# Mixer B's output projection and norms moved into its chunk loop, its first norm into the stage before, and one activation table for logarithm and exponential

## The chip, the cores and the metric

The program runs on one core of a Trainium2 chip. Such a core has five engines with a queue of instructions each: TensorE (PE, matrix products into the accumulator memory, here `ps`, eight banks of 128 x 512 float32), VectorE (DVE), ScalarE (ACT, functions by table), GpSimd (POOL) and SyncE (SP, which issues transfers). They run beside each other and wait for each other by semaphores. The metric is the time on the device in microseconds (us), the median of several runs.

## The reference

Four blocks follow each other, each on `x = x + block(layernorm(x))`, with `x` of 2 x 1024 tokens by 128 channels: mixer A (a selective state-space scan with state 16), an FFN with a shared expert and eight routed ones, mixer B, and the same FFN again. The change is about mixer B, cut here to what matters:

```python
h = rmsnorm(u, norm_w)                    # u = layernorm(x)
z, xBC, dt = split(h @ in_proj_w.T)       # 256 | 512 | 4 channels
xBC = silu(conv4(xBC) + conv_b)           # xs (4 heads x 64), B (128), C (128)
dt = softplus(dt + dt_bias);  A = -exp(A_log)
step: h = h * exp(dt*A) + dt * x (outer) B;   y = h @ C    # over 128 tokens
y = y + D * xs
y = rmsnorm(y * silu(z), ssm_norm_w)
x1 = u + y @ out_proj_w.T
h = rmsnorm(x1, post_norm_w)
return x1 + (silu(h @ gate_w.T) * (h @ up_w.T)) @ down_w.T
```

The residual of the network adds this to `x`.

## The kernel before

Everything lies as channels on the 128 partitions and T = 2048 tokens in the free dimension, worked on in four pieces of CH = 512 tokens (`cols(c)`, NCH = 4). Five stages follow each other, each one a block with one hand-written list of instructions per engine: loading, `mixer_a_stage` (0 to 280.5 us in the trace), `ffn_stage` with tag f (to 641.3), `mixer_b_stage` (641.6 to 818.9) and `ffn_stage` with tag g. No scheduler sets an order: each engine runs its list in the order of the code, and semaphores join the lists. A function of the same name often stands in the lists of several engines.

Mixer B, in the order of its lists. `Norm` (lines 188 to 233) centres x by a matmul (L194), squares it on ACT (L204), sums by a matmul (L188), and makes two logarithms a piece on ACT: the joint one (layer norm and RMS norm in one, L212) and the plain one (L214); then exponentials (L218, L221) and multiplications on DVE (L233) and POOL. The projections (L1787, L1810) follow, and DVE's convolution (L2205, L2208) in six passes. Then the chunk loop: TT = 16 chunks of 128 tokens. `chunk_inputs(c+1)` on PE makes the decay exponents and transposes of the next chunk (L1836, L1825, L1827, L1844 to L1846), ACT's `chunk` exponentiates (L2004, L2009, L2011) and `keep` decays the state (L2016), DVE's `prepare` and `next_state` mask, scale and add (L2240 to L2267), POOL scales the values by dt (L2189) and builds the step matrices two chunks ahead (L2160), and `chunk_outputs(c)` on PE makes y of the chunk (L1860, L1861) and its state (L1864). Behind every fourth chunk `gate_y` on DVE (L2274, L2282) adds D*xs and multiplies by silu(z), ACT squares (L2024), PE sums the squares (L1873, `mean_squares`), and ACT saves the sum (L2028).

Behind the loop come the output projection (`project_out`, L1879), logarithm and exponential for both norms (L2093 to L2118), the residual (L2327, L2329), the sum of its squares (L1943), the scaling (L2333), the split of the input into a high and a low part for rounded matmuls (`high_of_x` L2032, `low_of_x` L2287), and the MLP in NQ = 12 steps: gate and up matmuls (three passes each, L1884 to L1886), silu (L2128), product (L2344), and two steps later the down matmuls.

ACT's functions come in table sets, and a change of set is an instruction of its own, ACT_TABLE_LOAD. Log stands in the set `natural_log`, exp in `exp_and_others`, silu in `silu_and_others`. In the whole program there are 42 such loads.

In an FFN stage, a shared expert runs in a loop over q (`down(q - 2)`), then 39 tiles of gathered rows run through the experts: POOL gathers rows by indirect transfers, `turn_row` transposes them on PE (L1141), and ACT and DVE make silu(gate)*up (L1299, L1618) for the two halves of each tile. DVE's `add(2)` (L1579) is the last addition of the shared expert.

## Time and profile before

| what | value |
|---|---|
| runs, us | 1187.43, 1183.34, 1183.73 (median 1183.73) |
| profiled execution, us | 1191.55 |
| its span, first to last instruction | 1189.7 |
| busy PE / DVE / ACT / POOL, us | 994.6 / 742.7 / 601.5 / 594.8 |
| mean granted clock of PE | 0.923 of full |
| instructions | 16179 |
| mixer B from its first instruction | 641.6 to 818.9 us of the span |

The span is the time from the first to the last instruction; the execution's own time is 1.85 us longer. Busy time is the sum over an engine's instructions. Idle time is put down to what ended it ("<-"). A granted clock of 1.00 is 2.4 GHz, of 0.50 it is 1.2 GHz. `x4` behind a row says that so many equal instructions that follow each other are in it, with the sum of their time. A float32 matmul is two passes, each counted as one.

### The profile page before, as it was taken

The numbers are of one execution on the slowest core, as the hardware profiler recorded it, in microseconds if no ns is written. First come the engines' busy times: TensorE is split into PE (matmuls) and PEld (weight loads), VectorE is DVE, ScalarE is ACT, GpSimd is POOL, SyncE is SP. The second block draws the span as 40 slices with busy tenths as digits, with TensorE's granted clock in tenths as the row PEclk, the third lists the DMA queues.
The fourth block names the chain that finished last, engine by engine and source line by source line (L and its number), as shares of the span: only waits on it lengthen the run. The fifth ranks groups of instructions, "written<-read, shape, count | busy, mean of one in ns | idle before, by whom it ended". The sixth has DMA issues, their size and how long they took to land. (4 is left out here: it accounts for less than half of the span.)

```text
span 1189.7 us, 16179 instructions
## 1 busy us (share of the span) xinstructions
PE 994.6 (84%) x4707; PEld 704.7 (59%) x4707; DVE 742.7 (62%) x1197; ACT 601.5 (51%) x1129; POOL 594.8 (50%) x465
## 2 busy tenths in 40 slices
PE   5889999988996779973997888878996679993698
PEld 2323333335666669973985456455665669993696
DVE  4899999995873436641655866554683336651466
ACT  5675657656332435531556766667432335551353
POOL 2388988995048653364114746211128543547212
PEclk8999899989998889995999879988998889996899
DMA  4222222335011231121004000004111212111003
GB/s 131 64 72 71 82 80 83 96 92 170 19 59 38 71 70 52 54 73 35 15 12 111 1 1 1 1 0 135 54 60 28 77 31 90 56 52 51 19 12 113
DMA packets 60399, 69.40 MB, mean 58 GB/s; under 512 B 6232, under 2 KB 42848, under 8 KB 60320
## 3 DMA queue, kind: packets, MB, share of 16 engines
q1 hardware_dynamic: 55328, 58.15, 16.2%
q0 software_dynamic: 4992, 10.23, 3.3%
q8 instruction: 46, 0.75, 0.3%
q14 instruction: 33, 0.27, 0.1%
HBM read 57.74 MB, written 10.62 MB: 57 GB/s over the span
## 5 line engine op out<-in xcount | busy, mean ns | idle before, releaser
L764 POOL TENSOR_TENSOR a_hc<-a_h,a_c_sb 128x512 f32<-128x512 f32 x128 | 159.5, 1268 | 41.0 <-DVE a_h L672 40.9
L449 PE MATMUL ps<-a_hc,eye 128*128 128x512 f32 x256 | 133.6, 637 | 9.8 <-POOL a_hc L764 8.8
L589 ACT ACTIVATE ps<-a_delta,a_neg_a 128x512 f32<-128x512 f32 x128 | 87.3, 688 | 64.1 <-DVE a_h L672 63.5
L1126 PE MATMUL ps<-f_ring_rounded,f_q_hi_rounded 128*128 x312 | 81.8, 352 | 25.7 <-DVE f_q_hi_rounded L1591 17.2
L1126 PE MATMUL ps<-g_ring_rounded,g_q_hi_rounded 128*128 x312 | 80.3, 347 | 22.4 <-DVE g_q_hi_rounded L1591 22.4
L449 PEld LDWEIGHTS ps<-a_hc,eye 128*128 128x128 f32 x256 | 45.1, 194 | 77.1 <-POOL a_hc L764 40.1
L1618 DVE TENSOR_TENSOR g_prods<-g_work,ps 128x470 f32<-128x470 f32 x78 | 50.1, 644 | 53.7 <-remote 32.1
L672 DVE TENSOR_TENSOR_SCAN a_h<-ps,a_state,a_b_u 128x512 f32<-128x512 f32 x64 | 78.7, 1266 | 3.8 <-ACT ps L589 3.6
L1126 PEld LDWEIGHTS ps<-f_ring_rounded,f_q_hi_rounded 128*128 128x128 f32 x312 | 62.1, 199 | 29.6 <-issue 27.1
L1618 DVE TENSOR_TENSOR f_prods<-f_work,ps 128x470 f32<-128x470 f32 x78 | 50.0, 644 | 46.3 <-remote 23.4
L672 DVE TENSOR_TENSOR_SCAN a_h<-ps,a_b_u 128x512 f32<-128x512 f32 x64 | 75.2, 1207 | 3.1 <-ACT ps L589 2.9
L1299 ACT ACTIVATE g_work<-ps 128x470 f32<-128x470 f32 x78 | 43.8, 563 | 65.8 <-remote 35.7
L1126 PEld LDWEIGHTS ps<-g_ring_rounded,g_q_hi_rounded 128*128 128x128 f32 x312 | 61.0, 196 | 26.3 <-issue 23.8
L974 POOL CAST g_ring_rounded<-g_ring 128x1876 fp32r<-128x1876 f32 x8 | 14.0, 1754 | 122.5 <-DMA g_ring<-in_dn 122.5
L1299 ACT ACTIVATE f_work<-ps 128x470 f32<-128x470 f32 x78 | 43.7, 564 | 54.9 <-PE ps L1157 31.6
L1108 PE MATMUL ps<-eye,g_prods 128*128 128x128 f32 x312 | 44.1, 288 | 32.4 <-DVE g_prods L1618 32.4
L1003 POOL DMA_INDIRECT token_rows<-f_rows,f_back x39 | 37.8, 968 | 66.9 <-DVE f_rows L1597 59.1
L1003 POOL DMA_INDIRECT token_rows<-g_rows,g_back x39 | 37.4, 960 | 64.0 <-DVE g_rows L1597 55.9
L652 DVE TENSOR_TENSOR a_b_u<-a_du,ps 128x1024 f32<-128x1024 f32 x57 | 68.0, 1194 | 0.1
L1587 DVE TENSOR_TENSOR g_q_lo_rounded<-ps,g_q_hi_rounded 128x512 fp32r<-128x512 f32 x78 | 45.8, 620 | 34.5 <-ACT g_q_hi_rounded L1276 20.0
L995 POOL DMA_INDIRECT g_rows<-xn_rows,g_source x39 | 37.0, 949 | 58.2 <-DVE g_source L1545 47.1
L1155 PE MATMUL ps<-f_ring_rounded,f_work_rounded 128*128 x156 | 63.9, 409 | 1.7 <-issue 0.9
(483 smaller groups left out, 2902.5 us busy)
## 6 DMA issues: line engine op xcount, KB each, us to landing
a_c_sb<-c_rows SPq DMA_DIRECT2D x64, 256.0 KB, 3.2
f_ring<-in_gu SPq DMA_DIRECT2D x16, 469.0 KB, 4.3
g_ring<-in_gu SPq DMA_DIRECT2D x16, 469.0 KB, 4.2
f_ring<-in_dn SPq DMA_DIRECT2D x8, 512.0 KB, 5.9
g_ring<-in_dn SPq DMA_DIRECT2D x8, 512.0 KB, 5.6
xn_rows<-f_work SPq DMA_DIRECT2D x8, 256.0 KB, 3.6
f_rows<-token_rows SPq DMA_DIRECT2D x8, 256.0 KB, 5.2
xn_rows<-g_work SPq DMA_DIRECT2D x8, 256.0 KB, 2.8
```

The source lines that it names most:

```text
L449: nc.tensor.matmul(ps[:, Y + f, :], k.eye[:, :], hc[:, s % WAITING, :], start=False, stop=(n == NST - 1)).then_inc(y_added, 1)
L589: nc.scalar.activation(ps[:, A + m % NA, :], delta[:, f, cols(g)], ACT.Exp, scale=neg_a[:, f, n:n + 1])\
L652: nc.vector.tensor_tensor(decayed_in[:, p:p + FT, :], du[:, :, cols(g)], ps[:, B + i % 2, :].unsqueeze(1).to_broadcast([P, FT, CH]), ALU.m ...
L672: nc.vector.tensor_tensor_scan(h[:, s % DEPTH, :], ps[:, A + m % NA, :], decayed_in[:, m % FEED, :], initial, ALU.mult, ALU.add).then_inc( ...
L764: nc.gpsimd.tensor_tensor(hc[:, m % WAITING, :], h[:, s % DEPTH, :], c_sb[:, i % RING, :], ALU.mult)\
L1003: nc.gpsimd.indirect_dma_start(k.token_rows, bass.IndirectOffsetOnAxis(ap=back[:, j:j + 1], axis=0), rows[:, j, :], None).then_inc(sent, 16)
L1108: last = nc.tensor.transpose(ps[:, TR + i // 4, (i % 4) * P:(i % 4 + 1) * P], prods[:, j % 2, i * P:(i + 1) * P], k.eye[:, :])
L1126: last = nc.tensor.matmul(ps[:, Y2, 0:2 * P], q_hi[:, j % 2, a], in_ring(place, w, w + 2 * P), start=(i == 0), stop=(i == NI), skip_group_ ...
L1155: nc.tensor.matmul(out, xt[:, 0, j % 2, :], w_hi, start=True, stop=False)
L1299: nc.scalar.activation(gates[:, half, 0:HALVES[half]], ps[:, 2 * half, 0:HALVES[half]], ACT.Silu)\
L1587: last = nc.vector.tensor_tensor(q_lo[:, j % 2, a], ps[:, TR + half, 0:n], q_hi[:, j % 2, a].bitcast(F32), ALU.subtract)
L1618: nc.vector.tensor_tensor(prods[:, j % 2, half * H0:half * H0 + HALVES[half]], gates[:, half, 0:HALVES[half]], ps[:, 2 * half + 1, 0:HALVE ...
```

## The change

It has six parts.

- One table set, `LOG_EXP`, holds logarithm and exponential, and takes the place of the other two everywhere in both mixers. There are 22 table loads then.
- Mixer B's first norm (centring, squares, sums, joint logarithm) runs at the end of stage f, in the lists `centre_next`, `variance_next`, `square_next`, `log_next`, with f's additions as its input. Mixer B's weights are loaded there too, on SP. The plain norm's logarithm comes in the convolution, its exponential in chunks 0 to 3, the multiplication on POOL there.
- The output projection, both norms and the residual run inside the chunk loop, piece by piece. There are five pieces: 512, 512, 512, 256 and 256 tokens, which end with chunks 4, 8, 12, 14 and 16 (`PIECES`, `ENDS`). The sums, the projection and the variance of one piece use one bank in turn (`turn_of`).
- The last chunk's state, which nobody reads, isn't made.
- The multiplication in `gate_y` is one instruction over both banks.
- In both FFN stages `turn_row(0)` stands one step earlier on PE, and DVE's `add(2)` stands ahead of the waits for the first tile's second half.

```diff
+LOG_EXP = "natural_log_exp_and_others"
...
     (ffn_stage, PE)
+                if q == NPRE - 1:
+                    turn_row(0)
                 if q >= 2:
                     down(q - 2)
-            turn_row(0)
...
     (ffn_stage, DVE)
                 for half in range(2):
+                    if j == 0 and half:
+                        add(2)
                     dve.wait_ge(gates_silu, 2 * j + half + 1)
                     dve.wait_ge(ups_ready, 2 * j + half + 1)
-                    if j == 0 and half:
-                        add(2)
...
     (end of ffn_stage f, ACT)
+            if following is not None:
+                def square_next(c):
+                    act.wait_ge(next_centred, c + 1)
+                    nc.scalar.activation(work[:, cols(c)], ps[:, NEXT_CENT[c], :], ACT.Square).then_inc(next_squared, 1)
+                def log_next(c):
+                    act.wait_ge(next_var, c + 1)
+                    nc.scalar.activation(following.joint[:, cols(c)], ps[:, NEXT_VAR[c], :], ACT.Ln, bias=k.eps[:, 2:3])
...
     (mixer_b_stage)
+    PIECES = [slice(c * CH, (c + 1) * CH) for c in range(NCH - 1)]
+    PIECES += [slice(T - CH, T - CH // 2), slice(T - CH // 2, T)]
+    ENDS = (4, 8, 12, 14, 16)
+    def turn_of(p):
+        return ps[:, S if p == ALL - 1 else M, 0:width(p)]
...
     (PE)
+            def variance(p):
+                pe.wait_ge(res_done, p + 1)
+                pe.wait_ge(n_squared, p + 1)
+                nc.tensor.matmul(turn_of(p), k.ones[:, :], y[:, 0, PIECES[p]], start=True, stop=True)\
+                    .then_inc(n_ready, 1)
             for c in range(TT):
                 if c + 1 < TT:
                     chunk_inputs(c + 1)
+                if c in (8, 12):
+                    variance(c // 4 - 2)
                 chunk_outputs(c)
-                if c % 4 == 2 and c > 4:
+                if c in (4, 8, 12):
                     mean_squares(c // 4 - 1)
+                if c in (5, 9, 13):
+                    project_out(c // 4 - 1)
+                if c == 14:
+                    variance(2)
+            mean_squares(3)
+            gate_up(0)
+            project_out(3)
+            mean_squares(4)
+            gate_up(1)
+            project_out(4)
+            variance(3)
+            variance(4)
...
     (ACT, behind chunk(c) and keep(c - 1))
+                if c < NCH:
+                    act.wait_ge(plain_log, 1)
+                    nc.scalar.activation(rms[:, c, :], rms[:, c, :], ACT.Exp, scale=-0.5).then_inc(plain_ready, 1)
+                if c in (9, 13):
+                    rstd_n(c // 4 - 2)
+                if c in (5, 9, 13):
+                    square(c // 4 - 1)
+                if c in (6, 10, 14):
+                    rms_of(c // 4 - 1)
+                if c in (7, 11, 15):
+                    square_n(c // 4 - 1)
+                if c in (10, 14):
+                    high_of_x(c // 4 - 2)
+            square(3); rstd_n(2); rms_of(3); square(4); rms_of(4)
+            square_n(3); rstd_n(3); square_n(4); rstd_n(4)
             nc.scalar.preload_act_table_set("silu_and_others")
+            high_of_x(2)
...
     (DVE, behind next_state(c + 1))
-                if c % 4 == 3:
+                if c in (3, 7, 11):
                     gate_y(c // 4)
+                if c == 13:
+                    gate_y(3)
+                    residual(2)
+                if c in (5, 9):
+                    residual(c // 4 - 1)
+                if c in (9, 13):
+                    scale_in(c // 4 - 2)
+                if c in (10, 14):
+                    low_of_x(c // 4 - 2)
+            gate_y(4); scale_in(2); residual(3); residual(4)
+            low_of_x(2); scale_in(3); scale_in(4)
```

How the lists look now at two places. First ACT around chunks 9 and 10 (an exponential, a copy and an exponential, then `b_kept`, are one chunk). Before, a square stood ahead of chunk 9, and chunks 9 and 10 followed each other:

```order
L2024 ACTIVATE b_sq<-b_y 128x1024
L2004 ACTIVATE ps<-ps 128x512
L2009 ACTIVATE b_toks<-ps 128x384
L2011 ACTIVATE ps<-ps 128x512
L2016 ACTIVATE b_kept<-b_state,b_e_end 128x64 x4
L2004 ACTIVATE ps<-ps 128x512
L2009 ACTIVATE b_toks<-ps 128x384
L2011 ACTIVATE ps<-ps 128x512
L2016 ACTIVATE b_kept<-b_state,b_e_end 128x64 x4
```

After, from the end of chunk 9 (line numbers of the changed kernel: L2136 and L2138 are `rstd_n`, L2120 `square`, L2125 and L2127 `rms_of`, L2142 `high_of_x`):

```order
L2112 ACTIVATE b_kept<-b_state,b_e_end 128x64 x4
L2136 ACTIVATE b_raw_b<-ps,eps 128x512
L2138 ACTIVATE b_raw_b<-b_raw_b 128x512
L2120 ACTIVATE b_sq<-b_y 128x1024
L2100 ACTIVATE ps<-ps 128x512
L2105 ACTIVATE b_toks<-ps 128x384
L2107 ACTIVATE ps<-ps 128x512
L2112 ACTIVATE b_kept<-b_state,b_e_end 128x64 x4
L2125 ACTIVATE b_rms<-ps,eps 128x512
L2127 ACTIVATE b_rms<-b_rms 128x512
L2142 ACTIVATE b_sz_rounded<-b_xp 128x512
```

Six instructions stand between chunks now, three behind chunk 9 and three behind chunk 10; of these only the square was in the loop before.

Second, PE at the loop's end. Before, behind the last chunk's y and state: all projections, the last sum of squares, all variances, then the MLP:

```order
L1861 MATMUL ps<-b_c_in,b_state 64x128
L1864 MATMUL ps<-b_x_end,b_toks 128x256
L1879 MATMUL ps<-b_y,b_w_out 128x512 x6
L1873 MATMUL ps<-b_sq,half 128x512 x2
L1879 MATMUL ps<-b_y,b_w_out 128x512 x2
L1943 MATMUL ps<-b_y,ones 128x512 x4
L1884 MATMUL ps<-b_sz_rounded,b_w_hi 128x512
```

After (L1951 `mean_squares`, L1970 to L1972 one product of the MLP, L1959 `project_out`, L1966 `variance`):

```order
L1937 MATMUL ps<-b_c_in,b_state 64x128
L1951 MATMUL ps<-b_sq,half 128x256 x2
L1970 MATMUL ps<-b_sz_rounded,b_w_hi 128x512
L1971 MATMUL ps<-b_sz_rounded,b_w_hi 128x512
L1972 MATMUL ps<-b_sz_rounded,b_w_lo_rounded 128x512
L1970 MATMUL ps<-b_sz_rounded,b_w_hi 128x512
L1971 MATMUL ps<-b_sz_rounded,b_w_hi 128x512
L1972 MATMUL ps<-b_sz_rounded,b_w_lo_rounded 128x512
L1959 MATMUL ps<-b_y,b_w_out 128x256 x2
L1951 MATMUL ps<-b_sq,half 128x256 x2
```

The projections of three pieces are gone from here; the last two pieces, of half width, stand between the products of the MLP's first two steps.

## Rows read from the trace of the kernel before

**Rows 1.** Windows: from:to, length, busy us of PE, PEld, DVE, ACT, POOL, then PEclk.

```profile
346.00:619.00 273.00, 220.84 (x1401) 203.11 (x1400) 129.54 (x275) 111.18 (x235) 134.14 (x101) 0.89 0.16 46
...
694.00:765.00 71.00, 62.82 (x444) 44.77 (x445) 45.93 (x96) 46.62 (x119) 37.64 (x44) 0.95 0.00 1
765.00:819.00 54.00, 42.38 (x136) 27.55 (x134) 28.19 (x44) 36.17 (x57) 5.07 (x4) 0.91 0.00 0
```

**Rows 2.** Time line, 19 to 23 us: start, length, line, count, [idle before <-releaser].

```profile
19.89 1.28 ACT L218 ACT_TABLE_LOAD   x1
21.19 2.19 ACT L218 ACTIVATE a_du<-a_du 128x512 f32<-128x512 f32 x4
...
22.79 1.19 PE L351 MATMUL ps<-a_xp,a_w_tap 128*128 128x512 f32 x1 [5.11 <-DVE a_xp L233]
```

**Rows 3.** Waits of DVE, 40 to 310 us: us in total, times, longest.

```profile
DVE a_h L672 <- ACT ps L589: 6.6, 6, 2.0
```

**Rows 4.** Time line in mixer A's scan loop, 150 to 153 us.

```profile
150.62 1.28 ACT L568 ACT_TABLE_LOAD   x1
...
152.64 1.28 DVE L672 TENSOR_TENSOR_SCAN a_h<-ps,a_state,a_b_u 128x512 f32<-128x512 f32 x1 [2.04 <-ACT ps L589]
```

**Rows 5.** Chain that ended last, first norm of g: start, length, what.

```profile
823.67 1.28 ACT L1245
```

**Rows 6.** Time line, first expert tile of stage f.

```profile
352.21 0.69 DVE L1579 TENSOR_TENSOR x<-x,ps 128x512 f32<-128x512 f32 x1 [1.32 <-PE ps L1157]
...
353.04 0.30 PE L1141 MATMUL ps<-eye,f_rows 128*128 128x128 f32 x1 [0.93 <-DVE x L1579]
```

**Rows 7.** Time line, beginning of mixer B.

```profile
641.60 1.28 ACT L206 ACT_TABLE_LOAD   x1 [4.09 <-PEq L922]
...
650.96 1.28 ACT L218 ACT_TABLE_LOAD   x1
...
653.75 3.75 PE L1787 MATMUL ps<-b_xp,b_w_in 128*128 128x512 f32 x4 [5.00 <-DVE b_xp L233]
...
657.54 1.28 DVE L2205 TENSOR_SCALAR b_bc<-ps,vec 128x1024 f32<-128x1024 f32 x1 [2.14 <-PE ps L1787]
```

**Rows 8.** Page, part 5: costliest groups (count | busy, mean ns | idle before).

```profile
L764 POOL TENSOR_TENSOR a_hc<-a_h,a_c_sb 128x512 f32<-128x512 f32 x128 | 159.5, 1268 | 41.0 <-DVE a_h L672 40.9
```

**Rows 9.** Time line of TensorE in the chunk loop.

```profile
708.64 0.38 PE L1836 MATMUL ps<-b_bc 128*128 128x128 f32 x2
...
711.83 0.38 PE L1836 MATMUL ps<-b_bc 128*128 128x128 f32 x2
...
715.12 0.45 PE L1860 MATMUL ps<-b_mix,b_x_dt 128*64 128x128 f32 x4 [1.65 <-DVE b_y L2282]
```

**Rows 10.** Windows in the chunk loop, columns as in rows 1.

```profile
696.30:702.70 6.40, 6.39 (x28) 4.91 (x29) 3.18 (x8) 2.62 (x7) 4.66 (x6) 0.50 0.00 0
702.70:715.00 12.30, 10.77 (x88) 8.04 (x86) 9.14 (x20) 7.29 (x21) 7.83 (x9) 1.00 0.01 2
```

**Rows 11.** Time line, tail of mixer B and first steps of its MLP.

```profile
760.44 0.44 PE L1861 MATMUL ps<-b_c_in,b_state 128*64 128x128 f32 x4
...
761.35 5.31 PE L1879 MATMUL ps<-b_y,b_w_out 128*128 128x512 f32 x12
...
774.69 5.20 PE L1943 MATMUL ps<-b_y,ones 128*128 128x512 f32 x8 [4.60 <-ACT b_y L2111]
...
787.15 0.60 ACT L2128 ACTIVATE b_gate<-ps 128x512 f32<-128x512 f32 x1 [0.58 <-PE ps L1886]
...
788.20 0.63 PE L1884 MATMUL ps<-b_sz_rounded,b_w_hi 128*128 128x512 f32 x1
...
788.62 0.63 PE L1885 MATMUL ps<-b_sz_rounded,b_w_hi 128*128 128x512 f32 x1
...
791.96 0.60 ACT L2128 ACTIVATE b_gate<-ps 128x512 f32<-128x512 f32 x1 [0.65 <-PE ps L1886]
```

**Rows 12.** Waits of TensorE in f's expert tiles: us in total, times, longest.

```profile
PE ps L1108 <- DVE f_prods L1618: 23.7, 4, 16.0
```

More of the change, by code:

```diff
@@ L789, in mixer_a_stage, with ffn_stage @@
     return counters, spent
-def ffn_stage(k, d, which, tag, cleared, ready, out=None, logs=None):
+def ffn_stage(k, d, which, tag, cleared, ready, out=None, logs=None, following=None):
     nc, ps = k.nc, k.ps
@@ L2048, in keep_next @@
                 nc.scalar.activation(logs[:, c, :], ps[:, NEXT, :], ACT.Copy).then_inc(next_read, 1)
-            norm.of_scalar(act)
-            act.wait_ge(loaded, 48)
+            for c in range(NCH):
+                nc.scalar.activation(xp[:, cols(c)], xp[:, cols(c)], ACT.Exp, scale=-0.5).then_inc(joint_ready, 1)
             nc.scalar.activation(neg_a[:, :], head_rows[:, 1, :], ACT.Exp).then_inc(a_ready, 1)
@@ L2082, in _ @@
             for c in range(TT):
-                if c % 4 == 1 and c > 4:
-                    square(c // 4 - 1)
-                if c % 4 == 0 and c > 4:
-                    save(c // 4 - 2)
                 chunk(c)
@@ L2120, in _ @@
+                if c in (10, 14):
+                    high_of_x(c // 4 - 2)
+            square(3)
+            rstd_n(2)
+            rms_of(3)
+            square(4)
+            rms_of(4)
+            square_n(3)
+            rstd_n(3)
+            square_n(4)
+            rstd_n(4)
             nc.scalar.preload_act_table_set("silu_and_others")
-            high_of_x(1)
+            high_of_x(2)
             for q in range(NQ):
```

327 lines of the change are left out of this document (185 added, 142 removed).

## The prediction

> **What bounds the kernel now.** I read the busy time by stretch first [rows 1]: the expert tiles of f alone are 273 us (those of g as much), and the change hardly touches them. In mixer B's chunk loop (694 to 765) TensorE is busy 62.8 of 71 us, in the tail and MLP behind it 42.4 of 54. So the loop has little room to take work and the tail has much idle time to give. Then, engine by engine, the waits and the time lines around each edit, to see which engine everybody waits for there; each table load in them is 1.28 us.
>
> The sum is made against the profiled execution, 1191.55 us (span 1189.7 and 1.85 around it). The median of the three timed runs is 1183.73, 7.8 less; the terms below are differences, and I put them on the median.
>
> **Table loads with one log/exp set (42 become 22).** A load costs time only where it stands on the path.
> Start of mixer A: Ln ends at 19.88, load until 21.17, Exp, DVE's scaling, and TensorE had been idle for 5.11 us at 22.79 [rows 2]. All in one chain: -1.3. The two loads before the first scan (39 and 42 us) have ACT slack in front of them: 0.
> In mixer A's scan loop DVE sets the pace. It waited for ACT's L589 six times, 6.6 us in all, once 2.04 at 152.64 [rows 3, 4]. That one stands right behind two loads (the second at 150.62) that go; their 2.56 exceed the wait. The same pair precedes a wait of 0.19 and one of 0.61. These three add to 2.8, and I take -2.8. The other three waits stand behind silu loads and the next norm's work, which stay. Bounds: 0 if other ACT work or POOL's multiplies (159.5 us [rows 8]) are what ends a round, -6.6 if all waits went.
> The loads at mixer A's end lie beside DVE work, and so does the one in f's first norm: 0. In g that norm's load is on the path: in the chain that ended last the load stands from 823.67 to 824.95 [rows 5]. -1.3 (bounds 0 and -1.3).
>
> **Add and turn moved in the FFN stages.** At tile 0 DVE's add (L1579) sat behind the wait for the second half: it began at 352.21 after 1.32 idle, and TensorE waited 0.93 for it [rows 6]. Ahead of the waits it fills that idle time; L1618 then starts some 0.65 sooner, since the next instruction starts 0.60 behind the add's start. -0.7 in each of f and g, -1.4 together (0 to -1.9, twice the wait). The gather behind turn_row(0) is governed by its DMA, not by the matmuls around it: 0, at worst 0.3 each way.
>
> **Mixer B's first norm at the end of f.** Before, the block begins with a load (641.60); behind squares and Ln comes a second load (650.96), Exp, DVE's scaling, TensorE's projections (3.75 for four, half clock) and at 657.54 DVE's convolution [rows 7]. After, centring can start behind f's last transposes, some 1.4 sooner, since only the additions of f are needed; both loads are off the chain (the first preloads while ACT waits, as ACT had idled 4.09). The four joint Ln no longer have the four plain ones (0.57 each) between them, but the block's change now falls between Ln and Exp, and DVE does two copies of 0.7 and w_in 0.6 ahead of its scaling. My walk, an estimate: logs end at 647.85, 0.35 for the block's change, Exp 648.2, scaling from 650.05, convolution from 653.9 at full clock or 654.65 at half. 657.54 - 654.65 = 2.9. Bounds -1 (if the change of block costs 2 more) and -3.7 at full clock. The plain norm's Ln lies beside DVE's convolution, and its multiply goes to POOL in chunks 0 to 3, 1.27 us each by the 128x512 multiplies of [rows 8]. POOL is busy 7.83 of 12.30 us in the second row of [rows 10]; four more make 12.9, just too much, but POOL has idle time before the loop: 0 to +0.8, taken as 0 within the loop's term.
>
> **The chunk loop takes the output projection and norms.** A steady chunk is 3.18 us (708.64 to 711.83) with TensorE back to back [rows 9], so each matmul put in is paid: three projections 5.31 (twelve passes, 0.44 each [rows 11]); three variances at two passes 2.6; one dropped state matmul -0.5; the three mean_squares only move. That is +7.4 of TensorE alone. Then waits. PE now asks for square(p) right behind chunk 4p+4 and for variance(p) at 8 and 12, while ACT has square, Ln, Exp and high_of_x queued between its chunks, and DVE residual, scale_in and low_of_x. ACT's in-order queue is the danger: high_of_x at c=10 waits for scale_in, behind it stand the three exponentials of chunk 11, and for these wait DVE's mix and TensorE. Walking the queues with the durations of such rows gives groups of four chunks longer by 1.7, 3.4 and 5.4 us to the last y: +10.5, of which 2.65 is one wait of TensorE, for square_n(2) ahead of variance(2). The gate, for which TensorE sat idle 1.65 at 715.12, stays. Bounds: +6 if DVE's single 128x1024 multiply and shorter idle times before chunks give some back; +20 if each of the nine pieces of ACT and DVE work (3 x square, Ln/Exp, residual) pushes its chunk by its own 1.1 to 1.4 us.
>
> **The tail.** Before: last y ends about 760.85, first silu of the MLP (L2128) at 787.15, 26.3 us [rows 11]. In it are the projections (5.31), four loads (5.1) and a round of eight Ln, eight Exp and residuals at full width, with TensorE idle 4.60 in front of the variances. After it, counted from the last y: gate of half a piece 1.7; TensorE meanwhile does mean_squares(3) and gate_up(0), six passes at 0.43 (788.20 to 788.62, clock at half there), then project_out(3) and mean_squares(4), to 5.3; Ln and Exp at half width 0.9; two DVE halves 1.0; square 0.4; variance and its wait 0.6; Ln and Exp 0.9; silu load 1.28; high_of_x 0.6; first silu at 11.45 (sum with handovers of 0.5). That is -14.85. The first two MLP steps' matmuls are then done: before, the third silu came 4.81 behind the first, after 3.5: -1.3. Bounds of the two together: -12 (each handover 0.3 more, everything at half clock) and -18 (full clock, and the ACT queue short).
>
> **Sum.** -1.3 - 2.8 - 1.3 - 1.4 - 2.9 + 10.5 - 14.85 - 1.3 = -15.35. 1183.73 - 15.35 = 1168.4. I say 1168.5 (for the profiled execution 1176).
>
> **Two rules of the skill.** A load is followed at once by the next instruction: load from 19.89, 1.28 long, Exp at 21.19 [rows 2]. The Trainium skill, "ScalarE: Activation LUTs", section "What ACT_TABLE_LOAD costs", gives the same 1.28 us for the load but adds a drain of about 1.38. By it each of six loads on the path (one at the start, one at mixer B's front, three net in the tail, one in g) would give 1.38 more, an estimate of -23 to -24 in all; the row shows no such gap, and I don't count it.
> Idle TensorE has cost its clock here: the stretch 696.3 to 702.7, behind the convolution in which TensorE had little to do, ran at 0.50, 1.2 GHz, and its chunk took 6.4 us instead of 3.18; the chunks behind it ran at 1.00, 2.4 GHz, and the idle 1.65 at 715.12 is followed by passes of full speed [rows 9, 10]. The Trainium skill, "TensorE: Matmul & The Clock Gate", section "HAM oscillation — how this bites in real kernels", warns that stalls inside a loop can throw the engine back to half rate again and again; this speaks against putting waits in the loop and is the second rival.
>
> **Rivals.**
> (1) The loop gives it all back: growth at its upper bound 20 and the tail at -12, with the other terms at -7: +1, so 1178 to 1187. For it: TensorE is busy 88% of the loop and ACT already 46.6 of 71 us [rows 1]. Against: ACT and DVE keep 24 and 25 us of idle time there, and each is asked to take some 12.
> (2) Slower: TensorE's clock falls in the loop. New waits stand at six places (squares at 4, 8, 12, variances at 8, 12, 14). Each fall costs 3.2 us as at 696.3. With +10.5 and -25.85 for the rest, five falls give +0.65, and at six with the loop's waits at their upper bound (+9.5) it is 1183.73 - 15.35 + 19.2 + 9.5 = 1197. It decides from five or six falls. Against: the three waits of 1.6 us there now cause none.
> (3) The expert stages shift. In f's expert tiles TensorE waits 23.7 us in four times for DVE, once 16.0 [rows 12], and in g likewise; DVE and ACT stand still there too. What sets them off isn't in the profile; if their number depends on where instructions fall, one more or less moves the time by 7 to 16 us, and the spread of the times (1183.3 to 1191.6) may be this. One less: 1152 to 1161; one more: 1176 to 1184.
> (4) The loads are hidden anyway: without the 5.4 us of table terms 1174.
>
> **How the numbers follow.** Forecast 0.5, rival 1 0.14, rival 2 0.05, rival 3 0.09 up and 0.07 down, rival 4 0.15. What a measurement can tell from no change is 0.5%, 5.9 us, so faster is below 1177.8. The forecast, rival 4 and the lower shift are faster (0.72), and of the upper shift about half: 0.77. Rival 1 mostly and the rest of rival 3: same 0.16. Rival 2 and the tail of rival 1: slower 0.07. The forecast's own terms sum to bounds of roughly -22 to -6; with the shifts and a part of rival 1 the range is 1157 to 1180.
>
> **What would show it.** ACT's loads 22, the DVE wait at 152 gone; the convolution 3 us sooner after f's last addition; from the last y to the MLP's first silu 11 to 12 us instead of 26; the loop from its first y to its last longer by 8 to 13 with a granted clock of 1.0; no idle TensorE of over 3 us in the tail. Wrong if the loop's stretches show a clock of 0.5, if TensorE waits over 3 us at the variances, or if the expert stretches differ from before's (273 us in f) by more than 3 us.

## The result, and the profile after

| | before | after |
|---|---|---|
| median of 16 timed runs, us | 1186.46 | 1178.24 |
| lowest and highest | 1179.95, 1193.67 | 1172.11, 1183.86 |
| span of the profiled execution | 1189.7 | 1182.1 |

The ratio is 0.993, with a 95% interval of 0.9908 to 0.9952: the change takes 8.2 us (5.7 to 10.9) where I had forecast 15.3. The sign was right and the size was not. (The forecast counted from 1183.73, the median of three runs; sixteen give 1186.46.)

I cut both traces at the same events and compare the pieces. The windows of the changed kernel, with its columns as in [rows 1], from y of chunk 0 to chunk 4, on to y of the last chunk, to the MLP's first silu, to its last matmul, to the first matmul of g's gate, and to g's first expert tile:

```profile
691.80:707.90 16.10, 14.12 (x109) 10.73 (x108) 10.69 (x22) 12.29 (x35) 15.74 (x18) 0.95 0.01 1
707.90:765.00 57.10, 48.61 (x319) 31.12 (x319) 38.34 (x74) 35.90 (x88) 27.11 (x31) 1.00 0.01 1
765.00:779.50 14.50, 10.28 (x49) 8.04 (x48) 3.87 (x8) 7.84 (x16) 3.02 (x3) 0.86 0.00 0
779.50:809.60 30.10, 29.01 (x104) 20.82 (x104) 19.00 (x32) 18.28 (x35) 0.00 (x0) 0.90 0.00 1
809.60:816.70 7.10, 3.78 (x9) 1.27 (x8) 1.39 (x3) 4.66 (x7) 0.00 (x0) 1.00 0.62 202
816.70:884.70 68.00, 65.47 (x270) 47.56 (x270) 48.92 (x99) 26.66 (x44) 15.64 (x10) 0.92 0.28 87
```

and the same pieces of the kernel before:

```profile
698.90:715.10 16.20, 14.57 (x109) 11.27 (x108) 10.69 (x23) 8.84 (x27) 10.29 (x12) 0.88 0.01 2
715.10:759.70 44.60, 39.88 (x300) 28.41 (x300) 29.57 (x63) 29.69 (x78) 24.59 (x29) 1.00 0.00 1
759.70:787.10 27.40, 17.19 (x51) 8.42 (x51) 10.96 (x17) 21.26 (x30) 5.07 (x4) 0.89 0.00 1
787.10:817.80 30.70, 30.47 (x114) 22.22 (x112) 19.14 (x31) 18.72 (x34) 0.00 (x0) 0.93 0.00 1
817.80:826.40 8.60, 3.82 (x10) 1.30 (x9) 1.47 (x3) 6.11 (x9) 0.00 (x0) 0.95 0.70 221
826.40:892.00 65.60, 63.72 (x270) 45.92 (x270) 48.86 (x99) 26.64 (x44) 15.74 (x10) 0.95 0.27 84
```

The loop from chunk 4 on went from 44.6 to 57.1 us; TensorE is busy 8.7 us more in it (48.6 against 39.9) and idle 3.8 us more. The tail went from 27.4 to 14.5, the MLP from 30.7 to 30.1, g's norm from 8.6 to 7.1, and the stretch behind that grew from 65.6 to 68.0 at a lower clock (0.92 against 0.95). In front of the loop, the new beginning of mixer B, which answers to [rows 7]:

```profile
645.34 2.19 ACT L2161 ACTIVATE b_xp<-b_xp 128x512 f32<-128x512 f32 x4 [0.33 <-PEq L924]
...
647.14 2.47 DVE L2422 TENSOR_TENSOR b_xp<-ps,b_xp 128x512 f32<-128x512 f32 x4
...
647.96 2.68 PE L1859 MATMUL ps<-b_xp,b_w_in 128*128 128x512 f32 x4 [3.69 <-DVE b_xp L2422]
...
650.73 1.27 DVE L2307 TENSOR_SCALAR b_bc<-ps,vec 128x1024 f32<-128x1024 f32 x1
```

DVE scales x 9.93 us after f's last transposes (637.21 to 647.14); before it was 12.71 (640.21 to 652.92). The convolution starts at 650.73, TensorE's four passes in front of it (2.68 us) at a length between the 1.96 of full and the 3.75 of half clock (both are shown with e1 and e8).

In the first mixer the wait of [rows 3] has shrunk, and two others beside it have grown; before, a_yz stood at 4.0 and a_b_u at none:

```profile
DVE a_yz L632 <- PE ps L452: 5.0, 6, 1.7
DVE a_h L670 <- ACT ps L588: 3.6, 3, 1.8
...
DVE a_b_u L650 <- PE ps L439: 0.8, 1, 0.8
```

And the waits of TensorE in the loop:

```profile
PE ps L1936 <- DVE b_y L2382: 3.2, 3, 1.3
PE ps L1966 <- ACT b_y L2132: 2.6, 1, 2.6
PE ps L1959 <- ACT b_rms L2125: 2.1, 3, 0.7
PE ps L1899 <- DVE b_mix L2346: 1.1, 2, 0.7
PE ps L1899 <- POOL b_steps_lo L2261: 0.9, 2, 0.5
```

The first is the gate, smaller than before (4.8, the same three). The second is the one I had expected at 2.65, ahead of variance(2). The 2.1 are new: three times 0.69 in front of a projection. So are the 0.9 for POOL.

At the end of the loop ACT, DVE and TensorE stand like this:

```profile
759.60 0.69 DVE L2395 TENSOR_TENSOR b_xp<-xn,b_raw_b 128x512 f32<-128x512 f32 x1
...
760.32 0.63 ACT L2142 ACTIVATE b_sz_rounded<-b_xp 128x512 fp32r<-128x512 f32 x1 [3.59 <-DVE b_xp L2395]
...
760.85 0.58 ACT L2100 ACTIVATE ps<-ps 128x512 f32<-128x512 f32 x1
...
763.21 0.62 ACT L2132 ACTIVATE b_y<-xn 128x512 f32<-128x512 f32 x1
...
763.97 1.10 PE L1966 MATMUL ps<-b_y,ones 128*128 128x512 f32 x2 [2.62 <-ACT b_y L2132]
...
764.99 0.64 PE L1936 MATMUL ps<-b_mix,b_x_dt 128*64 128x128 f32 x4
...
765.39 0.66 PE L1937 MATMUL ps<-b_c_in,b_state 128*64 128x128 f32 x4
...
774.27 0.43 DVE L2389 TENSOR_TENSOR ps<-ps,b_rms 128x256 f32<-128x256 f32 x1 [2.23 <-PE ps L1959]
...
777.67 1.28 ACT L2221 ACT_TABLE_LOAD   x1
...
779.50 0.58 ACT L2229 ACTIVATE b_gate<-ps 128x512 f32<-128x512 f32 x1
```

ACT's high_of_x (L2142) waits 3.59 us for DVE's scaling, and only behind it come the exponentials of the last chunk (L2100) and the square (L2132) that TensorE's variance (L1966) waits for. The two y passes at 764.99 and 765.39 take 0.64 and 0.66 instead of 0.45: the granted clock has fallen to half (0.53 from 765.0 to 766.9). In the tail the first silu (L2229) comes at 779.50, 12.6 us behind the last y, with DVE's residual at 774.27 and the load at 777.67 on its way, as in the forecast's walk. At the beginning of the MLP TensorE stands idle 3.53 us (to 780.22) for that silu, where I had allowed none over 3.

### The profile page after: what moved, and what is told of

Its sections match the earlier page's. It is cut to its first block and busy times, and to the rows that moved or that the text cites. A ratio compares the mean times of both kernels' runs of the same rounds, so it can differ in the third digit from the quotient of the medians.

```text
span 1182.1 us, 16202 instructions
## 1 busy us (share of the span) xinstructions
PE 1004.1 (85%) x4715; PEld 712.0 (60%) x4715; DVE 745.9 (63%) x1204; ACT 573.3 (49%) x1109; POOL 595.7 (50%) x465
## 5 line engine op out<-in xcount | busy, mean ns | idle before, releaser
L452 PE MATMUL ps<-a_hc,eye 128*128 128x512 f32 x256 | 135.0, 645 | 10.3 <-POOL a_hc L762 9.7
L1134 PE MATMUL ps<-f_ring_rounded,f_q_hi_rounded 128*128 x312 | 81.8, 352 | 23.4 <-DVE f_q_hi_rounded L1639 15.3
L452 PEld LDWEIGHTS ps<-a_hc,eye 128*128 128x128 f32 x256 | 46.3, 198 | 77.4 <-issue 38.7
L1645 DVE SCALAR_TENSOR_TENSOR g_rows<-ps,g_share,g_work 128x128 f32<-128x128 f32 x39 | 13.7, 350 | 87.5 <-ACT g_work L1310 84.8
L1163 PE MATMUL ps<-g_ring_rounded,g_work_rounded 128*128 x156 | 65.1, 417 | 0.5 <-issue 0.5
```

The lines of the kernel that those rows point to most:

```text
L452: nc.tensor.matmul(ps[:, Y + f, :], k.eye[:, :], hc[:, s % WAITING, :], start=False, stop=(n == NST - 1)).then_inc(y_added, 1)
L1134: last = nc.tensor.matmul(ps[:, Y2, 0:2 * P], q_hi[:, j % 2, a], in_ring(place, w, w + 2 * P), start=(i == 0), stop=(i == NI), skip_group_ ...
L1163: nc.tensor.matmul(out, xt[:, 0, j % 2, :], w_hi, start=True, stop=False)
```

## The experiments

Each is timed against the kernel before on its own chip. The chip of e1, e2, e3 and e6 runs both expert stages without the bursts of waits of [rows 12] (211 us instead of 273), so its times lie some 124 us lower; ratios and pieces outside those stages are comparable. e2 and e6 have two runs each, the others four to twelve. e6 leaves out half of three projections, so what it computes is not the result; it is there for its time alone.

| run | what | median, us | before, us | ratio (95%) |
|---|---|---|---|---|
| e1 | table set alone | 1048.83 | 1062.03 | 0.9892 (0.9863 to 0.9921) |
| e2 | changed kernel, two sets | 1085.14 | 1062.03 | 1.0221 (1.0175 to 1.0267) |
| e3 | changed kernel, queue order | 1047.87 | 1062.03 | 0.9883 (0.9853 to 0.9913) |
| e6 | changed kernel, half projections | 1048.46 | 1062.03 | 0.9875 (0.9838 to 0.9913) |
| e7 | changed kernel | 1178.17 | 1187.35 | 0.9927 (0.9900 to 0.9954) |
| e8 | table set alone | 1171.84 | 1187.35 | 0.9872 (0.9832 to 0.9911) |
| e9 | e3, later projections, silus first | 1174.00 | 1187.35 | 0.9871 (0.9826 to 0.9916) |
| e10 | e9, POOL's work spread | 1174.05 | 1187.35 | 0.9881 (0.9845 to 0.9918) |
| e11 | e3, silus first, POOL spread | 1166.43 | 1183.76 | 0.9861 (0.9832 to 0.9890) |
| e12 | e11, weights scaled in f | 1167.79 | 1183.76 | 0.9867 (0.9825 to 0.9909) |
| e13 | changed kernel without the loop's part | 1173.80 | 1186.57 | 0.9910 (0.9878 to 0.9942) |
| e14 | changed kernel | 1177.98 | 1186.57 | 0.9938 (0.9915 to 0.9960) |
| e15 | e13, POOL spread, silus first | 1170.91 | 1186.57 | 0.9889 (0.9857 to 0.9920) |
| e16 | e11 again | 1169.79 | 1186.57 | 0.9886 (0.9853 to 0.9919) |

The pieces of the traces, in us ("f to scaling" is from the end of f's last transposes to DVE's first scaling of x; the loop's parts run from y to y, the tail from the end of the last y, the last column from g's gate to its first tile; the last y itself stands in no column: 1.14 us, but 1.95 in after, 1.71 in e14, 2.03 in e7, e2 and e6):

| run | f to scaling | to convolution | chunks 0-4 | chunks 4-15 | tail | MLP | g's norm | g's front |
|---|---|---|---|---|---|---|---|---|
| before | 12.71 | 4.62 | 16.19 | 44.62 | 26.27 | 30.67 | 8.55 | 65.66 |
| after | 9.93 | 3.59 | 16.09 | 57.05 | 12.56 | 30.11 | 7.13 | 68.01 |
| e7 | 9.93 | 4.32 | 16.41 | 57.63 | 11.86 | 29.81 | 7.11 | 66.52 |
| e14 | 9.91 | 4.33 | 15.88 | 58.01 | 11.74 | 29.58 | 7.11 | 66.39 |
| e1 | 11.30 | 2.83 | 14.45 | 44.57 | 22.56 | 30.42 | 7.14 | 63.44 |
| e8 | 11.30 | 4.63 | 14.79 | 44.60 | 21.94 | 30.63 | 7.12 | 63.61 |
| e13 | 9.92 | 4.28 | 16.27 | 44.59 | 21.36 | 30.29 | 7.12 | 63.13 |
| e15 | 9.92 | 4.47 | 14.44 | 44.59 | 21.94 | 30.33 | 7.13 | 63.10 |
| e3 | 9.92 | 4.61 | 15.90 | 53.29 | 11.75 | 29.16 | 7.13 | 64.66 |
| e9 | 9.93 | 4.47 | 16.41 | 53.71 | 11.21 | 30.23 | 7.12 | 68.70 |
| e10 | 9.92 | 4.38 | 14.58 | 53.70 | 11.22 | 28.98 | 7.12 | 68.02 |
| e11 | 9.92 | 4.61 | 15.44 | 53.30 | 11.22 | 29.85 | 7.12 | 63.23 |
| e12 | 9.34 | 4.37 | 15.14 | 53.30 | 11.23 | 29.38 | 7.12 | 66.37 |
| e16 | 9.92 | 4.61 | 15.43 | 53.30 | 11.21 | 29.83 | 7.12 | 63.33 |
| e6 | 9.92 | 4.28 | 16.42 | 55.54 | 12.83 | 30.28 | 7.13 | 63.11 |
| e2 | 10.08 | 4.63 | 15.90 | 70.20 | 18.25 | 30.43 | 11.44 | 70.54 |

**e1 and e8, the table set alone.** The kernel before with one set and without the loads that this makes needless (22 are left):

```diff
-        nc.scalar.preload_act_table_set("natural_log")
+        nc.scalar.preload_act_table_set("natural_log_exp_and_others")
...
-                        nc.scalar.preload_act_table_set("exp_and_others")
```

> The kernel before with one log/exp table set and nothing else of the change: 22 table loads instead of 42, the order of before everywhere. The trace after showed only 1.6 us gained up to the first matmul of stage f, where I had forecast 4.1. Theory 1 (the loads were partly hidden, and the start differs by chance): f's first norm matmul 1.0 to 2.5 us earlier than in before's trace, the scan's waits for L589 down from 6.6 to about 3.6 us, TensorE's waits there up by about 1.5. Theory 2 (all of the forecast 4.1 is there, and the one trace of after was unlucky): 3.5 us or more earlier. In the tail of mixer B three loads stand on the chain: last y to first silu 22.3 to 23.8 instead of 26.3. The chunk loop unchanged within 0.3. All together 5 to 8 us below before, 1179 to 1182 by before's 1186.5.

> The kernel before with the one table set and nothing else, again, for the comparison with the changed kernel on the same chip. Expected 0.987 to 0.991 of before. Segments as in the first run of it: last addition of f's rows to the convolution 14 us, loop 60, tail 22.5.

Measured: 0.9892 and 0.9872, that is 11 and 15 us, more than the 5 to 8 expected and more than the whole change gives. The pieces say where. The tail shrinks by 3.7 and 4.3 (three loads are 3.8); f to scaling by 1.41, one load and 0.13; g's norm by 1.42. The first mixer's scan, from first scan to last, is 226.5 and 227.2 us instead of 228.7, and fourteen traces without those loads give 227.3 on average, so 1.4 and not 2.8: theory 1 of e1 on that point. The other sign fits less well: stage f began 3.1 us earlier in e1, between the two theories, and 6.6 in e8, in the range of theory 2. On average over the fourteen traces it is 3.2. The stretch from TensorE's first matmul (L351) to the first scan scatters, with the same instructions, from 19.4 (in e8) to 23.0 us, so one trace can't settle it. The beginning of mixer B in e1 and in e8:

```profile
588.07 2.48 DVE L233 TENSOR_TENSOR b_xp<-ps,b_y 128x512 f32<-128x512 f32 x4 [4.13 <-ACT b_y L218]
...
588.91 1.96 PE L1782 MATMUL ps<-b_xp,b_w_in 128*128 128x512 f32 x4 [3.59 <-DVE b_xp L233]
...
590.90 1.28 DVE L2200 TENSOR_SCALAR b_bc<-ps,vec 128x1024 f32<-128x1024 f32 x1 [0.35 <-PE ps L1782]
```

```profile
647.95 2.48 DVE L233 TENSOR_TENSOR b_xp<-ps,b_y 128x512 f32<-128x512 f32 x4 [4.29 <-ACT b_y L218]
...
648.79 3.75 PE L1782 MATMUL ps<-b_xp,b_w_in 128*128 128x512 f32 x4 [3.58 <-DVE b_xp L233]
...
652.58 1.28 DVE L2200 TENSOR_SCALAR b_bc<-ps,vec 128x1024 f32<-128x1024 f32 x1 [2.14 <-PE ps L1782]
```

The same four passes take 1.96 us in one trace and 3.75 in the other, behind the same idle time of 3.6. At full clock the convolution comes 2.83 behind the scaling and at half 4.63. The two traces are of different chips, but on e1's chip e3 and e6 have 4.61 and 4.28.

**e7, the changed kernel beside e8.**

> The changed kernel itself beside the one with the tables alone (next run). Theory 1 (the table set carries all of the gain, and moving the projection and norms into the loop gives nothing): loop, tail and MLP together were 117.8 us in the trace after and 113.2 with the tables alone, the moved first norm gives 0, the moved addition 0.7 in each FFN stage, so this one is 0 to 5 us slower than the tables alone. Theory 2 (my forecast: the moved parts are worth 16.15 + 2.9 + 1.4 - 10.5 = some 10 us, of which the tables alone can give at most 6): it is 4 us or more faster than the tables alone.

Measured 0.9927 against 0.9872 on the same chip, 6.3 us between the medians, the changed kernel the slower, somewhat more than theory 1's 0 to 5. The two intervals overlap a little (0.9900 to 0.9911), but the runs of the two kernels, compared with each other, differ by 6.2 us on average (95%: 2.1 to 10.4). e14 (0.9938) and the first timing (0.993) say the same of the changed kernel, and e1 of the tables. By the pieces the difference of the two traces is 5.9 us, and 2.9 of these stand in g's front, which none of the edits touches and whose clock was 0.95 against 1.00. Theory 1 in kind: what the change gives is the table set, and the moved parts take some of it back.

**e2, the moved parts without the one set.** One line:

```diff
-LOG_EXP = "natural_log_exp_and_others"
+LOG_EXP = "exp_and_others"
```

> The changed kernel with its logarithms and exponentials in two table sets again (61 loads instead of 22), the order of the change kept. If ACT's queue is what the loop with the norms in it hangs on (theory 1), the ten loads inside the loop (five pairs of 1.28) lengthen it by 8 to 13 us and the eight or so behind the last y lengthen the tail by 8 to 11 us: 1195 to 1205 us. If the loop is bound by TensorE alone and ACT has room for them (theory 2), the loop grows by less than 4 us and the whole is 1188 to 1194.

(The expected totals stand on before's 1186; on this chip they are 124 lower.) The loop took 88.1 us instead of 75.1, the tail 18.3 instead of 12.6: 13 and 6. The whole is 37 us slower than e3 and e6 on its chip and 23 slower than before, more than the 9 to 19 expected. In loop and tail TensorE waits 6.9, 6.3 and 6.3 us in front of mean_squares, variance and project_out. So ACT's queue has no room for loads there, and with two sets the move costs far more: theory 1, at its upper end in the loop and below it in the tail.

**e6, half of the projections in the loop.** It leaves out the other half of the first three.

```diff
-                for f in range(FT):
+                parts = range(FT) if p >= NCH - 1 else range(1)
+                for f in parts:
```

> The changed kernel with only the first half (f = 0) of each of the three projections inside the chunk loop; the second half is left out, so two passes of 0.43 each are missing three times, 2.6 us. Theory 1 (TensorE's passes put into the loop are paid one for one): first y to last y 2.2 to 3.0 us shorter than in after's trace (73.1). Theory 2 (the queues of ACT and DVE set the time of the loop): under 1 us shorter, and TensorE's waits longer by the rest.

The three chunks with a projection took 4.97, 4.96 and 4.97 us instead of 5.82, 5.82 and 5.83: 0.86 each, two passes of 0.43, paid one for one. From chunk 0 to the last y it is only 1.2 us less than in after's trace (71.96 against 73.14), because chunks 0 to 3 took 0.3 longer and the last step, with the wait for variance(2) in it, took 6.46 instead of 5.41. (Against e7 and e14 it is 2.1 and 1.9 less.) The total lies between the two theories; the passes follow theory 1.

**e3, the queue order at the loop's end.**

```diff
-                if c in (10, 14):
+                if c in (11, 15):
                     high_of_x(c // 4 - 2)
...
     (DVE; low_of_x in chunks 11 and 15 likewise)
+                if c in (9, 13):
+                    scale_in(c // 4 - 2)
                 if c == 13:
                     gate_y(3)
                     residual(2)
                 if c in (5, 9):
                     residual(c // 4 - 1)
-                if c in (9, 13):
-                    scale_in(c // 4 - 2)
```

> The changed kernel with two of its own steps moved inside the loop: DVE does scale_in ahead of gate_y and residual in chunks 9 and 13, and high_of_x and low_of_x stand in chunks 11 and 15 instead of 10 and 14, behind square_n. In the trace after, ACT stood 3.59 us at high_of_x in front of chunk 15, and TensorE then waited 2.62 us for square_n(2), after which its passes ran at half clock for some 4.5 us. Theory 1 (ACT's in-order queue makes that wait): the wait of 2.62 is gone or under 0.8, no half clock there, last y 2.5 to 4 us earlier. Theory 2 (the wait only moves to DVE's mix for the last chunk): last y within 1 us of the changed kernel's, TensorE idle in front of the last y instead.

Chunks 4 to 15 take 53.29 us instead of 57.05 to 58.01: 3.8 to 4.7 earlier, at or above the upper end of what was expected (2.5 to 4). Part of it stands at the end (the last step 3.43 instead of 5.42 in after), part at chunks 10 and 11 (3.18 and 5.11 instead of 4.38 and 6.07). TensorE's waits in loop and tail there:

```profile
PE ps L1936 <- DVE b_y L2382: 2.8, 3, 1.2
PE ps L1959 <- ACT b_rms L2125: 2.1, 3, 0.7
PE ps L1966 <- ACT b_y L2132: 2.0, 2, 1.4
```

The wait for L2132 is 0.63 in the loop (the other 1.4 are in the tail, as in the changed kernel), and the y passes behind it are at full clock. Theory 1. Loop, tail and MLP are 111.3 us then, 1.9 less than e1's 113.2, yet the timed ratio (0.9883) isn't told apart from e1's (0.9892) on the same chip.

**e9 and e10, later projections and spread POOL work.** e9 adds to e3:

```diff
+                if c in (6, 10):
+                    project_out(c // 4 - 1)
                 chunk_outputs(c)
...
-                if c in (5, 9, 13):
+                if c == 13:
                     project_out(c // 4 - 1)
...
     (DVE)
-                if c in (5, 9):
+                if c in (6, 10):
                     residual(c // 4 - 1)
...
     (ACT, ahead of the MLP loop, and DVE with low_of_x)
-            high_of_x(2)
...
     (MLP loop of ACT, and of DVE with low_of_x)
-                if q < 2:
-                    high_of_x(q + 3)
+                if q in (1, 2, 3):
+                    high_of_x(q + 1)
```

> The changed kernel with the queue order of e3, and two more moves: the projections of pieces 0 and 1 stand one chunk later on TensorE (ahead of chunk_outputs in chunks 6 and 10, DVE's residual in the same chunks), where ACT's Ln has long read the bank; and in the tail the first two silus stand ahead of high_of_x(2), which comes in MLP step 1. Theory 1 (the 0.69 in front of each projection is idle time for ACT's Ln, and TensorE's 3.5 at the MLP's begin is ACT's queue): the loop 1.2 to 1.6 us shorter than e3's 70.3, the time from the last y to the first silu 0.5 to 0.7 shorter than 11.75. Theory 2 (other waits take their place): both within 0.3 of e3's.

e10 adds to e9:

```diff
     (POOL)
-                if c < NCH:
-                    pool.wait_ge(plain_ready, c + 1)
+                if c % 4 == 0:
+                    g = c // 4
+                    pool.wait_ge(plain_ready, g + 1)
...
     (ACT and DVE: of `normed` only as much awaited as piece p needs)
```

> As e9, and POOL's four multiplications of the plain norm stand in chunks 0, 4, 8 and 12 instead of 0 to 3. With the table set alone chunks 0 to 3 take 3.18 us each and 14.45 to the fourth gate; with the multiplications in them e3 has 3.5 to 3.8 a chunk and 15.9. Theory 1 (POOL, with 3.96 us of work a chunk, sets the pace there): y of chunk 4 begins 14.5 to 15.0 us after y of chunk 0. Theory 2 (ACT's extra exponential does): still 15.5 or more. Over all this version should be the fastest: 4 to 7 us below the changed kernel.

The silus first gave 0.54 in the tail (11.75 to 11.21). The later projections gave 0.9 at chunks 6 and 10 each and lost 1.3 and 2.1 in front of chunks 8 and 12, where variance now waits for the later residual, of which the chunks behind gave back 0.6 each: 53.71 against 53.29, theory 2 in the loop and theory 1 in the tail. Spreading POOL's work brought chunks 0 to 4 from 16.41 to 14.58, which is the value of e15 (14.44) and e1 (14.45): theory 1 there. POOL in the changed kernel, chunk 1:

```profile
697.34 0.62 POOL L2288 TENSOR_TENSOR b_x_dt<-b_toks,b_dt 128x256 f32<-128x256 f32 x1
698.10 1.29 POOL L2294 TENSOR_TENSOR xn<-xn,b_rms 128x512 f32<-128x512 f32 x1 [0.15 <-ACT b_rms L2201]
699.35 1.04 POOL L2261 TENSOR_TENSOR b_steps_hi<-masks,b_dta_hi 128x512 fp32r<-128x512 f32 x1
700.35 1.04 POOL L2261 TENSOR_TENSOR b_steps_lo<-masks,b_dta_lo 128x512 fp32r<-128x512 f32 x1
```

0.62 + 1.29 + 1.04 + 1.04 with hardly an idle 0.15: 3.8 to 4.0 a chunk. As a whole e10 was 4.1 us below the changed kernel by the medians, as expected, but not the fastest: e9 has the same median, and the tables alone lie 2.2 lower.

**e11 and e12.** e11 is e3 with the silus first and the spread POOL work. e12 adds:

```diff
     (end of ffn_stage f, DVE)
-                for c in range(NCH):
+                for c in range(NCH - 1):
                     keep_centred(c)
+                dve.wait_ge(next_loaded, 48)
+                nc.vector.tensor_scalar(following.w_in[:, :], following.w_in[:, :], k.vec[:, VB_NORM:VB_NORM + 1],
+                                        (1.0 + 1e-6) ** -0.5, ALU.mult, ALU.mult)
+                keep_centred(NCH - 1)
```

> The parts of the earlier versions that paid, without the later projections, which did not (chunks 6 and 10 gained 0.9 each in e9, chunks 8 and 12 lost 1.3 and 1.9 against e3): scale_in first and high_of_x late as in e3, the two silus ahead of high_of_x(2), POOL's multiplications in chunks 0, 4, 8, 12. Theory 1 (the terms add): first y to last y 70.3 - 1.5 = 68.8 or less, last y to first silu 11.2, convolution to first y and the rest as in e10. With 0.9 less than e10: 0.985 of before, some 8 us faster than the changed kernel and 1 to 4 faster than the tables alone. Theory 2 (they don't add, a later wait takes them back): the loop 69.4 or more, not faster than the tables alone.

> As e11, and DVE scales mixer B's projection weights at the end of stage f, between two copies where it has waited 1.0 us for ACT, and no longer between the block's begin and the scaling of x. Theory 1 (the moved first norm is a chain in which DVE's copies and weights delay the scaling by 1.9): the last transposes of f to DVE's first scaling 9.3 instead of 9.9. The convolution follows 2.8 behind that at full clock of TensorE or 4.3 to 4.6 at half; which of the two comes, no theory here says. Theory 2 (ACT's exponential is what the scaling waits for): still 9.9.

e11's loop was 69.9, not 68.8, by the number in the range of theory 2: chunk 0 took 4.03 against 3.18 in e10 (the clock in chunks 0 to 3 was 0.94, against 1.00), and the rest is what was expected (53.30, as in e3). It measured 0.9861; the tables alone did not run on its chip. e12's scaling came 9.34 us behind the transposes instead of 9.92, as theory 1 has it; the time of the whole doesn't show it (0.9867).

**e13 to e16, the move into the loop by itself.** e13 is the changed kernel with before's loop and tail (`project_out`, the norms and `gate_y` as they stood, ACT's `save` with a wait for POOL's multiplications); e15 adds to it the spread (over chunks 0, 2, 4 and 6) and the silus first. On TensorE:

```diff
-                if c in (8, 12):
-                    variance(c // 4 - 2)
                 chunk_outputs(c)
-                if c in (4, 8, 12):
+                if c % 4 == 2 and c > 4:
                     mean_squares(c // 4 - 1)
-                if c in (5, 9, 13):
-                    project_out(c // 4 - 1)
-                if c == 14:
-                    variance(2)
```

> The changed kernel without its fifth part: one table set, the first norm at the end of f with its multiplications on POOL in chunks 0 to 3, the moved turn and addition; but the projection, both norms and the residual behind the loop in four full pieces, as before. Theory 1 (the move into the loop costs about what it gives): loop 62 us (60.4 and 1.6 for POOL), last y to first silu 22, to the MLP's end 30.4, together 114.5 against 117.7 of the changed kernel, so 2 to 5 us faster than it. Theory 2 (the move gives some 6 us, as forecast without the loads, and something else loses them): 5 us or more slower than the changed kernel.

> The changed kernel for the comparison on this chip: loop 75 to 76, tail 12, MLP 30; 0.991 to 0.995 of before.

> As e13, with POOL's multiplications in chunks 0, 2, 4, 6 and the first two silus of the MLP ahead of high_of_x(1), which comes in MLP step 1. Theory 1: chunks 0 to 4 take 14.5 us and the loop 60.5, last y to first silu 21.4, so 2 us faster than e13. Theory 2 (the move into the loop, tidied up as in e11, is worth having): still 1 to 3 us slower than e11, whose loop, tail and MLP take 111.

> e11 again on the same chip as the three before: loop, tail and MLP 110 to 111 us, 0.984 to 0.988 of before, the fastest of the four by 1 us or more if the terms of the traces add.

e13 is 4.2 us below e14 by the medians, within theory 1, though the intervals overlap (0.9878 to 0.9942, 0.9915 to 0.9960); the means of the two differ by 4.5 (95%: 0.1 to 9.0), and in the traces another 3.3 stand in g's front (63.13 against 66.39). By the traces loop, tail and MLP are 113.7 us without the move and 116.9 to 117.8 with it (e14, e7, after), so the move costs 3.3 to 4.1 there. Tidied up it takes 110.9 (e16), 1.5 less than e15's 112.5. The moved first norm, for its part, brings the scaling 1.4 us forward (e13 against e8), and its multiplications on POOL take 1.8 in chunks 0 to 3 until they are spread (e13 against e15). (In e15 the spread gave its 1.8 in chunks 0 to 4, and the silus first gave nothing: the tail was 21.94, not 21.4.) e15 and e16 measured 0.9889 and 0.9886, the same: the 1 us or more that was expected for e16 is below what these timings can tell, and its ratio lies a little above the expected 0.984 to 0.988. The fastest by its medians is e11 (0.9861 and 0.9886); it beats the changed kernel (8.2 us on the same chip, e16 against e14) and isn't told apart from the tables alone.

## Why the prediction came out wrong

The sum of before, term by term, against the traces of the changed kernel (after, e7, e14):

| term | forecast | measured |
|---|---|---|
| start of the first mixer | -1.3 | -1.4 on average (21.4 against 22.79 in fourteen traces, 20.5 to 22.2) |
| its scan loop | -2.8 | -1.4 |
| f's and g's addition | -1.4 | -0.7 in f and -0.6 in g (from turn_row(0) to the first L1108, after L1116: 6.76 to 6.07, 6.47 to 5.86) |
| first norm moved, to the convolution | -2.9 | -2.8 to the scaling; with the clock behind it -3.8, -3.1, -3.1 |
| loop, first y to the end of the last | +10.5 | +13.1, +14.1, +13.7 |
| tail to the first silu | -14.85 | -13.7, -14.4, -14.5 |
| MLP | -1.3 | -0.6, -0.9, -1.1 |
| g's norm | -1.3 | -1.4 |
| g's front | 0 | +2.4, +0.9, +0.7 |

**The steps that failed.** The second is the largest. First, "it waited for ACT's L589 six times ... these three add to 2.8, and I take -2.8". The wait did fall by 3.0 (6.6 to 3.6 in after, 3.0 in e7 and e8). But in the same trace DVE waited 1.0 more for TensorE's L452 and 0.8 for L439, waits for another engine that had been hidden behind the one that went. -3.0 + 1.0 + 0.8 is -1.2, and the scan took 227.5 instead of 228.7. A wait that vanishes is worth only the distance to the next engine. The bounds 0 and -6.6 held the value.

Second, the loop: "+10.5". Passes were priced rightly (e6: 0.86 for two), and so was the wait for square_n(2), 2.65 forecast and 2.62 measured. The walk had 1.7, 3.4 and 5.4 for the groups of four chunks; the traces have 1.9, 5.0 and 6.4 to 7.1. What it lacked are the 0.69 in front of each projection (2.1 us), high_of_x in chunk 10 (with the order of e3 chunks 10 to 12 take 13.7 instead of 15.5), the fall of the clock behind the wait of 2.62, by which y of the last chunk took 1.95 us in after's trace instead of 1.14, and POOL; a shorter wait for the gate (3.2 instead of 4.8) gave part of it back. With e3's order chunks 4 to 15 cost 8.7 us more than before, and not 12.4 to 13.4. For POOL I had worked out 12.9 us of work in 12.3 and then taken 0; e10 against e9 and e15 against e13 show 1.8 (14.58 against 16.41, 14.44 against 16.27). It does not show in before against after (16.19 and 16.09), because before's chunk 0 ran at half clock, 4.92 us, which the changed kernel mostly escaped: that the term came out near 0 there is luck. With the known lengths of the queues, the fault was to take a lead of POOL for granted whose size I had not read.

Third, the MLP and tail together: -16.15 forecast, -14.3 to -15.6 measured. The walk of the tail was right to half a microsecond in e7 (11.86 for 11.45) and 1.1 short in after's trace.

Fourth, g's front. The clock there is in no term. In the three traces of the changed kernel it is 66.4 to 68.0 us, in e9, e10 and e12 66.4 to 68.7, in before's 65.7, in e3's 64.7, and in e1, e8, e13, e15, e6, e11 and e16 63.1 to 63.6. The instructions are the same in all. So the changed kernel missed some 3 us that others got; why, no run shows.

The measured terms, averaged over the three traces, add to -1.4 - 1.4 - 1.3 - 3.3 + 13.6 - 14.2 - 0.9 - 1.4 + 1.3 = -9.0, inside the timed interval (-5.7 to -10.9). Against the forecast 3.1 of the missing 6.3 us are the loop's, 1.4 the scan's and 1.3 g's front's.

**What was wrong in the argument rather than in a number** is the shares. I had put the table set at 5.4 us and called "the loads are hidden anyway" a rival of 1174. I left out of that figure the three net loads in the tail (3.8) and the second load in front of mixer B (1.3), which stood in the terms of the moved parts, and the clock behind it. The tables alone are 11 to 15 us, and rival 4 ran the wrong way round: the moved parts were what gave nothing on balance. Rival 1 (the loop gives it back) is nearest to what happened: against e13 the move saves 8.8 to 9.6 in the tail and 0.2 to 0.7 in the MLP, and costs 12.5 to 13.4 in the loop from chunk 4 on, with 0.6 to 0.9 more at the last y. Rival 2 had its mechanism in the traces once (a clock fall behind a wait of 2.62), not six times, and its price was too high: I had taken 3.2 from the length of a window, while y to y chunk 0 of before took 4.92 instead of 3.18. Rival 3 did not occur between these two traces: TensorE waited 23.9 us in five times for f_prods in after's against 23.7 in four, and f's tiles took 289.9 against 291.6 us. But whether these bursts exist at all depends on the chip (e1, e2, e3, e6), and where they do, f's tiles scatter from 286.4 to 294.4 us.

The rules weighed beforehand: where loads stood on a chain the next instruction followed at once (0.01 us behind), so the drain of the Trainium skill, "ScalarE: Activation LUTs", section "What ACT_TABLE_LOAD costs", shows on no chain; f to scaling lost 1.41 us with one load of 1.28, the tail 3.7 and 4.3 with three. The warning of the Trainium skill, "TensorE: Matmul & The Clock Gate", section "HAM oscillation — how this bites in real kernels", holds for one place of the loop: in after's trace the granted clock was 0.53 behind the idle 2.62 us, and 1.00 over chunks 4 to 14 with their shorter waits.

## What to carry to other kernels

Price each part of a change with the others in place and without them, above all when one part makes the others possible: here the cheap part gave all of the gain, and the moved work in an engine-bound loop cost 13 us to save 10 behind it (9 with the queues put in order, as in e3). A loop in which TensorE is busy 88% of the time charged every pass at its full length; move work into it only where its own engine has waits of the same length, and put what nobody in the loop needs (high_of_x) last in the queue. When a wait goes, read the next engine's slack before booking it.

## What the runs showed of the hardware

- A set with both logarithm and exponential costs the same load (1.28 us) as one with either, and the activations ran at the same length (0.70 us for the joint Ln of 128x512, L212, before and in e1).
- Four equal projections behind equal idle time (3.59 and 3.58 us) ran once at 2.4 GHz and once at 1.2 GHz (1.96 and 3.75 us). The idle time just before does not settle which comes; what does is open, and the two traces are of different chips.
- g's front, the same instructions, takes 63.1 to 68.7 us with its granted clock (1.00 to 0.90). These two windows are of e8 and of e14:

```profile
814.60:878.20 63.60, 61.20 (x270) 43.48 (x270) 49.41 (x99) 26.62 (x44) 16.14 (x10) 1.00 0.30 93
```

```profile
811.00:877.50 66.50, 63.95 (x271) 46.16 (x271) 49.05 (x100) 26.64 (x44) 15.74 (x10) 0.95 0.29 90
```

- The chip of e1, e2, e3 and e6 and the chips of the other traces differ by some 60 us in each expert stage, with the same instructions. The windows of f's tiles in e1 and in e8:

```profile
347.80:559.80 212.00, 210.40 (x1418) 195.34 (x1418) 128.84 (x275) 111.36 (x233) 132.17 (x99) 1.00 0.21 59
```

```profile
342.20:619.70 277.50, 222.10 (x1418) 204.73 (x1418) 129.29 (x275) 111.53 (x233) 132.36 (x100) 0.89 0.16 45
```

TensorE's idle time is 1.6 us in one and 55 in the other, at a clock of 1.00 and 0.89. In e8 DVE and ACT stand still for up to 11.3 and 12.8 us at a time and TensorE waits up to 16.0. The cause is open; a gain that one chip shows in a stage with such bursts should be taken from the pieces outside them.
